# Pacing indirect transfers one per expert block, and a later combine, in a macaron block on one Trainium2 core

## The reference

```python
x = x + 0.5 * ffn(layernorm(x))          # x: 4 x 512 tokens, D = 128
x = x + attention(layernorm(x))          # causal, one head, S = 512
x = x + 0.5 * ffn(layernorm(x))
# ffn: mixture of 8 experts, top 2 of softmax(x @ router_w.T), weights renormalised
#   h = gelu(x @ w1[e])  (128 -> 512);  y = h @ w2[e]  (512 -> 128);  out = sum of gate * y
```

## Time and profile before

| | |
|---|---|
| median of the timed runs | 332.69 us (332.57 to 332.88, three runs) |
| span of the profiled execution | 421.0 us |
| its own time | not given apart from the span |
| TensorE busy in it, mean granted clock | 273.8 us (65%), 0.85 of full speed |
| VectorE / ScalarE / GpSimd busy | 152.5 / 139.4 / 140.6 us |

### The profile page before, as it was taken

One profiled execution on the slowest core, in us unless ns is written; L12 is line 12 of the kernel. 1 busy time (PEld: TensorE's weight loads), 2 busy tenths in 40 slices (PEclk: granted clock), 3 DMA queues, 4 the chain that ended last, 5 costly groups with the idle time before them and its releaser, 6 DMA issues.

```text
span 421.0 us, 7028 instructions
## 1 busy us (share of the span) xinstructions
PE 273.8 (65%) x1957; PEld 249.7 (59%) x1958; DVE 152.5 (36%) x687; ACT 139.4 (33%) x267; POOL 140.6 (33%) x159
## 2 busy tenths in 40 slices
PE   0505193499981599985356853699709999596930
PEld 0404183399981599963246531698709998595930
DVE  3583331222210067312497632556102222132234
ACT  1101231255540345542131412265205564243420
POOL 9047257200047200047200373000770005666550
PEclk9999996699995599998595985789866999798785
DMA  7971112522222112111000011011221222222115
GB/s 218 411 199 51 62 58 63 200 64 69 70 76 68 44 56 64 37 45 50 25 1 2 19 50 56 9 37 51 77 67 46 70 65 69 62 63 71 55 55 164
DMA packets 38520, 31.79 MB, mean 76 GB/s; under 512 B 5224, under 2 KB 34416, under 8 KB 38112
## 3 DMA queue, kind: packets, MB, share of 16 engines
q1 hardware_dynamic: 33744, 18.12, 15.2%
q0 software_dynamic: 4752, 13.40, 9.2%
HBM read 15.68 MB, written 15.81 MB: 75 GB/s over the span
## 4 chain that ended last, share of the span: by engine, by line
PE 52%; another core or an unknown queue 15%; DVE 12%; issue 11%; POOL 5%; ACT 3%; DMA 2%; DVEq 0%; POOLq 0%; ACTq 0%; SPq 0%
PE bank L890 20%; PE bank L879 19%; POOL slots_in L395 3%; PE bank L870 3%; DVE xs L707 2%; PE bank L832 2%; PE bank L847 2%; PE bank L939 2%; DVE stats L565 1%; PE bank L901 1%; DMA y_rows<-final_rows 1%; DVE xs L740 1%; DVE neg_max L731 1%; PE bank L902 1%
## 5 line engine op out<-in xcount | busy, mean ns | idle before, releaser
L890 PE MATMUL bank<-w_sb,act 128*128 x736 | 106.4, 291 | 49.5 <-issue 25.4
L890 PEld LDWEIGHTS bank<-w_sb,act 128*128 128x128 f32 x736 | 97.1, 206 | 52.0 <-issue 51.9
L879 PE MATMUL bank<-xT,w_block 128*128 128x128 f32 x736 | 108.3, 295 | 0.1
L879 PEld LDWEIGHTS bank<-xT,w_block 128*128 128x128 f32 x736 | 99.7, 210 | 0.9 <-issue 0.5
L468 ACT ACTIVATE act<-bank 128x512 f32<-128x512 f32 x92 | 54.9, 597 | 133.8 <-PE bank L879 68.9
L693 DVE COPY yb<-bank 128x128 f32<-128x128 f32 x92 | 26.7, 291 | 178.7 <-PE bank L890 109.7
L407 POOL DMA_INDIRECT y_rows<-slots_out,slot_of x48 | 46.0, 957 | 101.5 <-DMA slots_out<-yb 87.5
L462 ACT COPY w_block<-w_sb 128x512 f32 x92 | 56.4, 614 | 20.0 <-issue 20.0
L395 POOL DMA_INDIRECT slots_in<-xn,slot_of x32 | 30.9, 966 | 58.9 <-DVE slot_of L641 49.7
L418 POOL DMA_INDIRECT final_rows<-yb,row_of x23 | 22.8, 989 | 51.5 <-DVE row_of L683 38.7
L870 PE MATMUL bank<-ident,xb_numbered 128*128 128x128 f32 x92 | 28.2, 307 | 17.9 <-DMA xb_numbered<-slots_in 10.5
(11 more groups left out here) (104 smaller groups left out, 221.1 us busy)
## 6 DMA issues: line engine op xcount, KB each, us to landing
xb_numbered<-slots_in SPq DMA_DIRECT2D x69, 64.0 KB
slots_out<-yb SPq DMA_DIRECT2D x69, 64.0 KB
w_sb<-in_L_ffn_w SPq DMA_DIRECT2D x8, 512.0 KB, 8.1
slots_in<-zeros POOLq DMA_DIRECT2D x2, 1472.0 KB, 12.0
numbered_slots<-numbered POOLq DMA_DIRECT2D x1, 1483.5 KB, 5.5
xb_numbered<-numbered_slots SPq DMA_DIRECT2D x23, 64.5 KB
xs<-in_L_attn_x SPq DMA_DIRECT2D x4, 256.0 KB, 3.5
out<-xs SPq DMA_DIRECT2D x8, 128.0 KB
```

The source lines that it names most:

```text
L879: mm = nc.tensor.matmul(h_ps[k][:, q * P:(q + 1) * P], w1_block[k][:, q * P:(q + 1) * P], xT[c2 % UNROLL][:], start=True, stop=True)
L890: mm = nc.tensor.matmul(y_ps[k][:, 0:D], act[k][:, q * P:(q + 1) * P], w2_sb[:, bass.ds(at + q * D, D)], start=(q == 0), stop=(q == HC - 1))
```

## The change

GpSimd gets a wait in front of each indirect transfer of three of the bursts: transfer number i (0 to 15) waits until `xT_copied` has reached `pace_from` + i + 1, so that one leaves for each block copied. Scatter 1 is paced from block 0 of phase 0, gather 0 from block 26, scatter 3 from block 46, which is block 0 of phase 1. Scatter 0, gather 1, scatter 2 and what follows scatter 3 are not paced.

FIRST_COMBINE goes from 30 to 32, and a pair of group 0 is combined at every fourth step from there (32, 36, 40, 44) instead of at 31, 33, 35, 37. The branch for the pieces of the normalisation, q >= 4, goes by the same count.

```diff
-        FIRST_COMBINE = MAX_BLOCKS + LAG + UNROLL
+        FIRST_COMBINE = MAX_BLOCKS + LAG + 6
...
-            def scatter(r):
+            def scatter(r, pace_from=None):
...
                 for t in range(GT):
                     for k in range(TOP):
+                        if pace_from is not None:
+                            pool.wait_ge(xT_copied, pace_from + TOP * t + k + 1)
...
-            def gather(p):
+            def gather(p, pace_from=None):
...
                 for t in range(GT):
                     for k in range(TOP):
+                        if pace_from is not None:
+                            pool.wait_ge(xT_copied, pace_from + TOP * t + k + 1)
                         pool.indirect_dma_start(
...
             scatter(0)
-            scatter(1)
+            scatter(1, pace_from=0)
             pool.wait_ge(numbered_set, 2)
...
-            for p in range(GROUPS):
-                for _ in gather(p):
-                    pass
+            for _ in gather(0, pace_from=MAX_BLOCKS + LAG):
+                pass
+            for _ in gather(1):
+                pass
             scatter(2)
             pool.wait_ge(slots_numbered, 16)
             pool.wait_ge(second_copied, GT // 2)
-            scatter(3)
+            scatter(3, pace_from=BLOCKS)
...
-                q, odd = divmod(s - FIRST_COMBINE, 2)
+                q, r = divmod(s - FIRST_COMBINE, 4)
                 if s < MAX_BLOCKS:
                     next(pieces, None)
...
                 elif q >= GT // 2:
                     next(norm_pieces, None)
-                elif q >= 0 and odd:
+                elif q >= 0 and r == 0:
                     combine_and_count(0, pair_of(q))
```

## The result

| | before | after |
|---|---|---|
| median of six runs each, same chip | 332.78 us (332.37 to 333.25) | 335.63 us (334.56 to 336.97) |
| ratio, 95% interval | 1 | 1.0092 [1.0066, 1.0117] |
| profiled execution: time, span | span 421.0 us | 336.38 us, 334.6 us |

A forecast was written before the change was run, and what follows sets the result against it. The prediction took freezes to belong to the profile and work between the experts and attention to lie on the timed path. Normalisation +3.3 and clock +1.0 gave +4.3, from 332.69 to 337.0 us (case 335.5 to 338.7; full range 331.0 to 339.5).

The forecast's parts named there:

- Timed runs hardly freeze: Whole kernel: the stalls during transfer bursts, 90.8 or 98.9 us in the profile, belong to that profiled execution.
- the two estimates, 330.2 and 322.1: Span in us without freezes: 330.2 with 90.8 us of freezes taken out, 322.1 with every small gap too.
- The rival that bursts freeze timed runs: Indirect-transfer bursts stall timed runs too, so pacing wins 5.3 us at the upper end: 330.7 to 331.7 us; chance 0.19.
- The normalisation falls into the open, +3.3: Between phase 0's last y copy and attention: normalisation no longer runs beside blocks, so the first transposed half comes 3.3 us later.
- Clock +1.0 (0 to 2.7): Attention's projections: after TensorE's wait its clock is low for 3.7 us, half speed for about 1.9 us, +1.0 us.
- Second scatter, cost 0: Phase 0, paced from block 0: the sixteenth transfer lands with 5.3 us of slack, so pacing costs 0.
- What can pacing win? I take 0: All paced bursts: between 0 and 5.3 us to win in timed runs, taken as 0.
- First gather, cost 0: Phase 0, paced from block 26: rows land before each combine with 3.5 us of slack, so pacing costs 0.
- fourth scatter does nothing: Phase 1, paced from block 46: without freezes no gate binds its sixteen transfers, so no effect.
- late rows: Paced gather rows come late for the combine; VectorE waits at four places, about 1 us each: 341 us; chance 0.04.
- The second gather: End of first attention: as a rival, this gather already binds and swallows most of the +4.3: 333 us; chance 0.08.
- The profile after: Changed kernel's profiled span: 380 to 395 us, some 30 us of freeze gone in phase 0, some 6 in phase 1.

The follow-up runs named there:

- fillers: The changed kernel with 13 matmuls whose results nobody reads in front of the first transposes for attention: 334.73 us, 1.0051; with 24: 337.19 us, 1.0121.

## Why the prediction was right

Its sign, its likeliest case and its own range (335.5 to 338.7) held; 335.63 lies at the lower edge. In part that is luck: the two terms of the sum came out at 4.9 us together instead of 4.3, which alone would give 337.6, and a gain of some 1.8 that the sum had at nothing brought the time down again. By its steps:

- **"Timed runs hardly freeze"**: right, and shown. The unchanged kernel unfrozen spans 331.6; of the two estimates, 330.2 and 322.1, the first is the one that kept small gaps as part of the kernel. About 1.8 us lie around the span (336.38 - 334.6; 333.33 - 331.6), not the 9 to 15 that the prediction set beside its sum. The rival that bursts freeze timed runs falls with that, and with the fill alone moved, where the burst stays and costs nothing.
- **"The normalisation falls into the open, +3.3"**: right to 0.04 (3.34). Put back, the loss is gone; moved alone, it is there in full.
- **"Clock +1.0 (0 to 2.7)"**: the mechanism is right and the term was too small: 1.56, from nT to the first finished unit with and without fillers. It took 3.7 us of low clock and let 1.8 of them fall on waiting. The clock was still at the upper level while TensorE waited (1.00 in 145 to 149 us) and fell behind the wait, so the whole low stretch lay over work. A mean of 0.57 over 4 us is about 3.4 us at the lower level, and TensorE is busy 3.98 of the 4, so nearly half of those 3.4 us is lost. The Trainium skill, "TensorE: Matmul & The Clock Gate", section "HAM oscillation — how this bites in real kernels", blames idle gaps of TensorE for such drops; the fillers agree at the seam. It doesn't explain a second stretch that comes in some runs of one kernel only.
- **"Second scatter, cost 0" and "What can pacing win? I take 0"**: this is the step that failed, by 1.6 to 1.8 us. The prediction did list the fill behind the paced scatter, "some 3 us later than now" (4.7 by the profile), and asked only who needs its result. It didn't ask what the 1.5 MB do to the steps beside them. Where the fill stood they cost 1.84 us, by way of ScalarE's 3.17 us in front of a copy of weights. In the earlier trace rows this couldn't be seen, since the freezes lay over the very steps. The Trainium skill, "DMA: Bandwidth & Descriptors", section "Issuing engines are not separate DMA queues", has the transfers of all issuers on the same 16 engines; the trace agrees (the fill on all 16 of them for 3.1 us, with no packet of SyncE's queue moving). The prediction held it against indirect bursts alone, where it does nothing. Its other detail, that four transfers leave at once and the rest follow at 1.89 us, was a little off: eight leave at 1.26 us each before a gate binds.
- **"First gather, cost 0", "fourth scatter does nothing"**: right. VectorE never waits for a gathered row in phase 0, and scatter 3's gates are open. That drops the late rows.
- **The second gather** swallowed nothing: from the last y copy to the last finished unit it is 30.18 us, before 25.25, and the 4.9 between them are the gap and the clock.
- **The profile after**: the span of 380 to 395 was wrong. It took it for granted that a disturbed profile would be disturbed again. A shorter profile and a longer time did come together, but a second profile of the unchanged kernel is short as well, so this shows nothing about pacing. The gap, the pieces behind the last y copy and the low clock were there as named.

Sum with measured terms: -1.86 + 3.34 + 1.56 + 0.03 + 0.28 - 0.35 = +3.0, against +2.85 of the medians. The scatter of the runs is not explained in full: the changed kernel's six fall into three near 334.7 and three near 336.7 us at nearly the same mean clock, and only one of the latter was profiled. Block 5 of phase 0 is transposed up to 1.0 us earlier in one kernel than in another (58.77 to 59.80), and no run tells why. What ScalarE waits for while the fill moves stays open too.

## What to carry to other kernels

When waits are put on a queue, look at what stands behind them in the list and where it lands now: here the only gain of three paced bursts came from a bulk fill that slid 4.7 us, off a turn of ScalarE's loop, which nobody had aimed at, and moving that fill gives the same without them. And when a bulk transfer is blamed for a slow step, look for the engine that stood before it blames a load: here the loads were in time, and the wait was ScalarE's. A count such as `q >= 4` that comes of two constants moves everything that hangs on it: spreading the combine from every second to every fourth step pushed a normalisation, once free, in front of the next stage. And where a profile spans much more than the timed runs, take it again before any duration in it is used.

## What the hardware showed

- A profiled execution can be disturbed beyond any timed one: 421.0 against 331.6 us for the same kernel.
- One transfer of 1483.5 KB (6.1 us to land) had all 16 DMA engines for 3.1 us. A turn of ScalarE's loop that fell into it began with 3.17 us of standing (3.12 to 3.31 in four kernels) and cost TensorE 1.15 us in one wait; its other turns there began with 0.76 to 1.01 us.
- Sixteen indirect transfers back to back, one per 1.26 us, cost the blocks beside them nothing.
- TensorE's clock fell to 1.2 GHz after 3.37 us of idling, for about 3.4 us of full work; with the gap filled it stayed at 2.4 GHz there. In three profiles, one of them of the kernel with the gap filled, it fell at the end of the same attention, for about 1.4 us of loss.
